# A decoder layer on one core: the norms' mean added with its sign turned, and a shorter run of filler products ahead of the first turn

## The chip, the cores and the metric

The kernel runs on one core of a Trainium2 chip. A core has a matrix engine (TensorE; PE in the profile, its weight loads PEld), VectorE (DVE), ScalarE (ACT), GpSimd (POOL) and a queue engine (SP) that here only issues transfers. The metric is the device time of one execution, in microseconds (us); lower is better. Several executions of a kernel are timed, and their median is given.

## The reference

One decoder layer on x of shape (4, 512, 128) in float32, 16 heads of 8 channels. Cut to what matters:

```python
def _layernorm(x, axis=-1, eps=1e-05):
    m = jnp.mean(x, axis=axis, keepdims=True)
    v = jnp.var(x, axis=axis, keepdims=True)
    return (x - m) / jnp.sqrt(v + eps)
...
x = x + attn(_layernorm(x))            # causal self-attention, Wq Wk Wv Wp with biases
x = x + xattn(_layernorm(x), ctx_1024) # attention to 77 context tokens, with a mask
x = x + ffn(_layernorm(x))             # 8 experts, the best 2 of each token weighted
```

The softmax subtracts each row's largest score. There are 3 norms for each of 4 batches, so 12 norms of 512 tokens each.

## The kernel before

Tokens lie on the 128 partitions, 4 tiles (T = 4) of 128 tokens for a batch; channels lie along the free dimension. One norm of one batch is this work:

- VectorE takes the statistics (BN_STATS and BN_AGGR into `moments`, which holds mean and variance, L740 and L743; L748 and L751 for the first norm).
- GpSimd adds the epsilon to the variance (`var`, L483), raises it to the power of minus one half (`rstd`, L484), and then writes `normed`, one instruction for each of the 4 tiles of tokens (L493). Each of these is `tensor_scalar` with two operations: subtract the mean, multiply by `rstd`. Both are one number per partition, read from memory.
- TensorE turns the 4 tiles (L884, `turn_x`), and ScalarE copies them out as `normed_t` (L613). Projections follow: q, k and v for the first norm of a batch, the query of the second attention, or the gate and the experts.

```python
last = gp.tensor_scalar(normed[:, i % 2, t], state[:, b, t], moments[:, n, t, 0:1],
                        rstd[:, n, t:t + 1], ALU.subtract, ALU.mult)
```

The very first norm (batch 0) is done in two halves of 2 tiles, `first_stats` to `first_split_k` for half 0 and half 1. The first half's `normed` is written by VectorE (L757), the second half's by GpSimd (L477). The turn of a half is L912, and its projections are L918.

Projected q and k are cut into three bfloat16 parts each (high, middle, low). The high part is ScalarE's; the rest after it is GpSimd's subtraction (L458); the middle is ScalarE's cast (L652); the low is GpSimd's subtraction again (L464). SP copies the parts into `q_stack` and `k_stack`, six transfers for each (L339), in the order high, middle, low. For batch 0 this is done by halves, on VectorE in GpSimd's place. A `peak` step multiplies the stacks on TensorE (L962 and L967), and VectorE finds each row's largest score (L781). A `scores` step multiplies again with that maximum inside (L1008). ScalarE takes the exponential (L672), GpSimd clears what lies above the diagonal (L569), and TensorE multiplies by the values (L1024). Before the first `scores`, SP has to put the maxima into `q_stack` (L415).

What sets the order: a string `ORDER` has one letter for each step. Every engine walks the whole string and does its own part of each step, in that order, with semaphores between engines. So each engine's program is in order, and an instruction that waits holds back all behind it. The letter `w` is a filler (`warm`): one product of ones with ones, 128x512 in bfloat16 (L893), into a bank that nobody reads. It does no work of the layer. There are 118 of them: 29 ahead of the first turn, 30 between the projection of the context keys and the first `peak`, the rest in small groups. GpSimd's early program is the clearing of buffers (`clear` steps, L500 to L523) between the norms.

Of the kernel before, what the change touches and what calls it, by code (L numbers as in the profile page):

```python
# [11 lines left out]
ALU = mybir.AluOpType  # L12
# [3 lines left out]
B, S, D, H, E = 4, 512, 128, 16, 8  # L16
DH = D // H
S2 = 77
T = S // 128
# [32 lines left out]
def chains():  # L52
# [34 lines left out]


ORDER = (
    "aqaqPVPPPwwwwwwwwwwwwwwwwwwwwwwwwwwwwwaLLLbwwaPLqaPwqwwaqbaVcqaqKwwwwwwwwwwwwwwwwwwwwwwwwwwwwwweeebe"  # L90
    "cebebebPebwweeewwbcKeewKKeKwwweeKiewwwwwKeeicecefwsLesiwwsfsfsafswfisfsfsfsvfsvfssvvfsjsvvmbsfsdvjsf"
    "svfscvvfsfvsfdsmvmcffscmdfsfmvfjsmsmLmvsggjvsgvsgmgsgmgsgvsmgvsgndggksdgvsgsvAkAsvAsnsAvgsAvAdsgvnAs"
    "AnAsggvdgnsgvsgAsvgsknshsnvcxhxvxkhxvhoynxhxyxhnEhshnhxhdsholsEnshsvlhsyshsvvBsBdyBPEsBvBPsEsBvBBBvs"
    "hoEhshoBEshsvEoEshxoxhsovxohxyxhxyFxvloElsoEsxFEvsvosssvpyyssvvFspsvCsFsCvCCCvvpCCFCEpFzCFzpCtpFptzx"
    "xtxpxzypFxxypFxFxGytGpyttGGFwwwwzwwwwDtDGDDtDDwDDDGzGtzDtztxGGxxGxGyxxyxxtHytyHtHGHwwzHztHtHztzHwwww"
    "wHwwwHHtttwwwwwwwwwwwwwwHwwwwzztttztztttt"
)


# [73 lines left out]
def decoder_layer(nc, x, ctx_t, mask, wq, bq, wk, bk, wv, bv, wp, bp, xwq, xwk, xwv, xwo,  # L173
                  gate_w, gate_b, expert_w, expert_b, out):
    with ExitStack() as stack:
        def sb(name, shape, dt=F32):
            return stack.enter_context(nc.sbuf_tensor(name, shape, dt))
# [26 lines left out]
        state = sb("state", [128, B, T, D])  # L204
        stats = sb("stats", [128, 3 * B, T, 6])
        moments = sb("moments", [128, 3 * B, T, 2])
        var = sb("var", [128, 3 * B, T])
        rstd = sb("rstd", [128, 3 * B, T])
        normed = sb("normed", [128, 2, T, D])
# [219 lines left out]
        def _(pool):  # L429
            gp = nc.gpsimd  # L430
            chain = [0]

            def link(ins):
                chain[0] += 1
                ins.then_inc(pool_chain, 1)
                pool.wait_ge(pool_chain, chain[0])
# [10 lines left out]
            for i in range(2):  # L447
# [3 lines left out]
                last = gp.affine_select(out=v, in_=v, compare_op=ALU.not_equal, fill=1.0, base=-64, pattern=[[-1, 64]],  # L451
                                        channel_multiplier=1)
# [14 lines left out]
            for step in SCHEDULE:  # L467
                kind, b, k = step
                if kind == "first_stats":
                    t = slice(2 * k, 2 * k + 2)  # L470
                    pool.wait_ge(first_moments_ready, k + 1)
                    link(gp.tensor_scalar(var[:, 0, t], moments[:, 0, t, 1], LN_EPS, None, ALU.add))
                    gp.tensor_tensor(rstd[:, 0, t], var[:, 0, t], minus_half[:, t], ALU.pow).then_inc(first_rstd_ready, 1)
                elif kind == "first_norm" and k == 1:
                    pool.wait_ge(first_rstd_ready, 2)
                    for t in (2, 3):
                        last = gp.tensor_scalar(normed[:, 0, t], state[:, 0, t], moments[:, 0, t, 0:1],  # L477
                                                rstd[:, 0, t:t + 1], ALU.subtract, ALU.mult)
                    last.then_inc(first_norm_ready[k], 1)
                elif kind == "ln_stats":  # L480
                    n = 3 * b + k
                    pool.wait_ge(moments_ready, STATS[step])
                    link(gp.tensor_scalar(var[:, n], moments[:, n, :, 1], LN_EPS, None, ALU.add))  # L483
                    link(gp.tensor_tensor(rstd[:, n], var[:, n], minus_half[:], ALU.pow))  # L484
                elif kind == "ln_norm":
                    n = 3 * b + k
                    i = NORM[step]
# [2 lines left out]
                    elif i > 2:  # L490
                        wait_full(pool, ("turn_x", *NORMS[i - 3][1:]))
                    for t in range(T):
                        last = gp.tensor_scalar(normed[:, i % 2, t], state[:, b, t], moments[:, n, t, 0:1],  # L493
                                                rstd[:, n, t:t + 1], ALU.subtract, ALU.mult)
                    last.then_inc(norm_ready, 1)
                elif kind == "clear" and k == "causal":

                    for rows in (128, 64):
                        v = causal[0:rows]
                        link(gp.memset(v, 0.0))  # L500
                        last = gp.affine_select(out=v, in_=v, compare_op=ALU.is_ge, fill=FUTURE, base=64 - rows,
                                                pattern=[[0, 4], [-1, 128]], channel_multiplier=1)
# [11 lines left out]
                elif kind == "clear" and k == "rank":  # L514
                    for e in range(E):
                        last = gp.memset(rank[:, :, e:e + 1], float(E - e))
# [612 lines left out]
```

## Time and profile before

| | us |
|---|---|
| median of 3 executions | 279.18 |
| lowest and highest of them | 278.38 and 280.3 |
| the execution that was profiled | 278.69 |
| its span, first to last instruction | 277.0 |
| TensorE busy | 258.9 (93% of the span) |
| VectorE busy | 207.6 (75%) |
| ScalarE busy | 162.7 (59%) |
| GpSimd busy | 150.5 (54%) |

The times of rows below are from the start of the span. The profiled execution took 1.7 us more than its span. It lies 0.5 us below the median. A row's "idle before" is how long its engine had nothing to run before the first instruction of the row, and the name behind it is what ended that. Ends of TensorE's products are modelled, so that neighbouring rows overlap by a tenth or two of a microsecond.

### The profile page before, as it was taken

Reading aid. Unit: us, or ns where it says so; the run is one execution under the profiler, and the core shown is the slowest. Engines: PE = TensorE matmul, PEld = TensorE weight load, DVE = VectorE, ACT = ScalarE, POOL = GpSimd, SP = SyncE. Lnnn points to the kernel's source line nnn. Section 1 sums busy time; section 2 is a strip of 40 time slices with the busy share of each in tenths; the row PEclk is TensorE's granted clock in tenths of the full one; section 3 lists DMA queues with packets and bytes.
Section 4 is the critical chain, followed back from the end, with each engine's and each line's share of the span. In section 5 each row is a group of like instructions: output and inputs, shape, how many; then the busy total and the mean of one; then the engine's idle time right before and its main releaser. Section 6 shows DMA issues by size and latency. Waiting matters only on the chain.

```text
span 277.0 us, 6747 instructions
## 1 busy us (share of the span) xinstructions
PE 258.9 (93%) x2642; PEld 140.3 (51%) x2642; DVE 207.6 (75%) x406; ACT 162.7 (59%) x223; POOL 150.5 (54%) x266
## 2 busy tenths in 40 slices
PE   8999896899988999999999969999799999998993
PEld 2554442434544444453545525367455684586583
DVE  6489997867887989987979945899338973864651
ACT  4232624989866988799977979961592009501100
POOL 7999833758869665675667694625811070032000
PEclk9999999799999999999999999999999999999999
DMA  3453364000452313400310001300004100100101
GB/s 106 110 143 94 86 165 110 2 6 4 117 152 71 82 37 105 135 9 5 100 31 2 7 2 29 98 2 8 0 11 116 38 7 2 38 2 0 38 2 39
DMA packets 21635, 14.62 MB, mean 53 GB/s; under 512 B 2788, under 2 KB 21604, under 8 KB 21604
## 3 DMA queue, kind: packets, MB, share of 16 engines
q1 hardware_dynamic: 20324, 13.61, 18.1%
q10 hardware_dynamic: 1280, 0.59, 0.8%
q8 instruction: 21, 0.34, 0.5%
q14 instruction: 10, 0.08, 0.1%
HBM read 2.39 MB, written 1.05 MB: 12 GB/s over the span
## 4 chain that ended last, share of the span: by engine, by line
PE 64%; DVE 17%; POOL 11%; ACT 3%; issue 2%; DMA 1%; POOLq 0%; SPq 0%; ACTq 0%
PE banks L1024 12%; POOL normed L493 8%; PE banks L1087 7%; PE banks L893 7%; PE banks L1008 7%; DVE peaks L781 6%; PE banks L884 5%; PE banks L967 4%; PE banks L1046 4%; PE banks L877 4%; PE banks L962 3%; DVE xpeaks L788 3%; POOL rstd L484 2%; PE banks L1073 2%; PE banks L1035 2%
## 5 line engine op out<-in xcount | busy, mean ns | idle before, releaser
L781 DVE TENSOR_REDUCE peaks<-banks 128x2 f32<-128x1024 f32 (+3 forms) x88 | 95.2, 1122 | 16.4 <-PE banks L967 15.8
L672 ACT ACTIVATE probs<-banks 128x1024 f32<-128x1024 f32 x80 | 79.4, 1031 | 14.3 <-PE banks L1008 13.7
L569 POOL TENSOR_SCALAR_AFFINE_SELECT probs<-probs 128x512 f32<-128x512 f32 (+1 forms) x80 | 43.2, 545 | 35.2 <-ACT probs L672 35.1
L1024 PE MATMUL banks<-probs,v_s 128*32 128x256 f32 (+3 forms) x512 | 43.2, 440 | 0.0
L677 ACT ACTIVATE xprobs<-banks 77x1024 f32<-77x1024 f32 x32 | 31.0, 1017 | 9.7 <-PE banks L1035 9.6
L493 POOL TENSOR_SCALAR normed<-state,moments,rstd 128x128 f32<-128x128 f32 x44 | 35.0, 809 | 0.7
L893 PE MATMUL banks<-ones_b 128*128 128x512 bf16 x118 | 32.1, 411 | 2.4 <-POOL minus_half L439 1.4
L1008 PE MATMUL banks<-q_stack,k_stack 64*128 64x512 bf16 (+3 forms) x256 | 30.8, 306 | 3.0 <-DMA q_stack<-peaks_t 2.4
L1087 PEld LDWEIGHTS banks<-expert_w_s,scaled 128*128 128x128 f32 x256 | 29.6, 192 | 4.9 <-issue 4.6
L1087 PE MATMUL banks<-expert_w_s,scaled 128*128 128x128 f32 x256 | 32.1, 280 | 0.0
L967 PE MATMUL banks<-k_stack,q_stack 64*128 64x512 bf16 (+3 forms) x256 | 31.9, 301 | 0.0
L851 DVE TENSOR_TENSOR scaled<-banks,normed_t 128x1024 f32<-128x1024 f32 x16 | 19.4, 1218 | 10.5 <-PE banks L1073 10.4
L962 PE MATMUL banks<-causal,halves 64*128 64x128 bf16 (+3 forms) x352 | 26.0, 227 | 1.0 <-DVE peaks L781 0.8
L788 DVE TENSOR_REDUCE xpeaks<-banks 128x8 f32<-128x616 f32 x32 | 23.9, 792 | 1.9 <-PE banks L983 1.6
L962 PEld LDWEIGHTS banks<-causal,halves 64*128 64x128 bf16 x352 | 13.3, 96 | 23.2 <-DVE peaks L781 10.4
L893 PEld LDWEIGHTS banks<-ones_b 128*128 128x128 bf16 x118 | 11.7, 104 | 17.4 <-issue 5.5
L1024 PEld LDWEIGHTS banks<-probs,v_s 128*32 128x32 f32 x512 | 12.3, 108 | 15.5 <-issue 11.4
L1008 PEld LDWEIGHTS banks<-q_stack,k_stack 64*128 64x128 bf16 x256 | 9.9, 96 | 16.3 <-DVE peaks L781 4.8
L1046 PE MATMUL banks<-xprobs,xv_s 77*32 77x512 f32 x128 | 16.6, 602 | 0.0
L613 ACT COPY normed_t<-banks 128x512 f32<-128x512 f32 x11 | 6.2, 586 | 16.3 <-PE banks L884 16.3
L807 DVE TENSOR_TENSOR g_scores<-banks,gate_b_s 128x32 f32<-128x32 f32 x4 | 0.8, 192 | 19.1 <-PE banks L877 19.1
L483 POOL TENSOR_SCALAR var<-moments 128x4 f32<-128x4 f32 x11 | 2.7, 246 | 22.4 <-DVE moments L743 22.3
(172 smaller groups left out, 370.8 us busy)
## 6 DMA issues: line engine op xcount, KB each, us to landing
xq_stack<-parts_x SPq DMA_DIRECT2D x24, 128.0 KB, 2.4
q_stack<-parts_q SPq DMA_DIRECT2D x18, 128.0 KB, 2.5
k_stack<-parts_k SPq DMA_DIRECT2D x18, 128.0 KB, 2.5
out<-state SPq DMA_DIRECT2D x4, 256.0 KB, 2.2
state<-in_x SPq DMA_DIRECT2D x3, 256.0 KB, 2.9
q_stack<-parts_q SPq DMA_DIRECT2D x12, 64.0 KB, 2.0
expert_w_s<-in_expert_w SPq DMA_DIRECT2D x1, 512.0 KB, 4.4
xk_stack<-parts_x SPq DMA_DIRECT2D x6, 77.0 KB
```

Source lines behind the costliest of these rows:

```text
L493: last = gp.tensor_scalar(normed[:, i % 2, t], state[:, b, t], moments[:, n, t, 0:1], rstd[:, n, t:t + 1], ALU.subtract, ALU.mult)
L569: gp.affine_select(out=v, in_=v, compare_op=ALU.is_ge, fill=0.0, base=0, pattern=pattern, channel_multiplier=-1).then_inc(causal_done, 1)
L672: ac.activation(probs[:, grp % 2, u], two_banks(step), ACT.Exp, scale=SCALE).then_inc(taken_by_act, 1)
L677: ac.activation(xprobs[0:S2, n % XPROBS], two_banks(step)[0:S2], ACT.Exp, scale=SCALE).then_inc(taken_by_act, 1)
L781: ve.tensor_reduce(peaks[:, f, t, :, a:a + n], two_banks(step)[:, :, 0:n * width].rearrange("p s (h k) -> p s h k", h=n), X_AXIS, ALU.max, ...
L788: ve.tensor_reduce(xpeaks[:, t, :, a:a + n], two_banks(step)[:, :, 0:n * S2].rearrange("p s (h k) -> p s h k", h=n), X_AXIS, ALU.max, nega ...
L893: te.matmul(bank(step), ones_b[:, 0:128], ones_b[:], start=True, stop=True)
L962: te.matmul(diagonal[:, s, :, 64 * i:128], halves[r, i], causal[r, 0:n, 0:128 - 64 * i], start=(i == 0), stop=False, skip_group_check=True)
L967: last = te.matmul(two[:, s, width * h:width * h + width], q_stack[r, b % 2, 4 * f + a + h, 128 * t:128 * t + 128], k_stack[r, b % 2, 4 * ...
L1008: last = te.matmul(two[:, s, col:col + n], k_stack[r, b % 2, p, 128 * kt:128 * kt + 128], q_stack[r, b % 2, p, 128 * kt:S], start=True, st ...
L1024: last = te.matmul(home[32 * c:32 * c + 32, 128 * kt:S], weight.rearrange("p a b -> p (a b)"), probs[:, half, unit, c % 2, col:col + S - 1 ...
L1087: last = te.matmul(home[:, D * t:D * t + D], scaled[:, (4 * b + k) % SCALED, i, 128 * t:128 * t + 128], expert_w_s[:, 2 * k + i], start=Fa ...
```

## The change

First, the norms. A new buffer `shift` holds the mean times minus one. GpSimd makes it with one more `tensor_scalar` for each norm, ahead of `var`, and for the second half of the first norm. `normed` on GpSimd is then `state` plus `shift`, times `rstd`: ALU.add stands where ALU.subtract stood, and `shift` where `moments` stood. 44 instructions in `ln_norm` and 2 in the second half of the first norm change so; 12 small ones are new. The first half's norm, on VectorE, stays.

Second, the fillers. `ORDER` without its `w` letters is the same string. Of the `w`, 15 of the 29 ahead of the first turn are gone, and so are 2 ahead of the last of the four first projections. New ones are 4 ahead of the turn of batch 1's first norm, 2 ahead of a pair of turns (the last norm of batch 1 and the second norm of batch 2), 1 ahead of the turn of batch 3's second norm, and 2 more (7 for 5) ahead of the turn of the last norm. 2 more have moved past a neighbouring step without a TensorE part. 118 become 110. No bank of a real step changes.

```diff
 ORDER = (
-    "aqaqPVPPPwwwwwwwwwwwwwwwwwwwwwwwwwwwwwaLLLbwwaPLqaPwqwwaqbaVcqaqKwwwwwwwwwwwwwwwwwwwwwwwwwwwwwweeebe"
...
+    "aqaqPVPPPwwwwwwwwwwwwwwaLLLbwwaPLqaPwqaqbaVcqaqKwwwwwwwwwwwwwwwwwwwwwwwwwwwwwweeewwwwbecebebebPebwwe"
...
+        shift = sb("shift", [128, 3 * B, T])
...
                     pool.wait_ge(first_moments_ready, k + 1)
+                    if k == 1:
+                        gp.tensor_scalar(shift[:, 0, t], moments[:, 0, t, 0], -1.0, None, ALU.mult)
...
                     for t in (2, 3):
-                        last = gp.tensor_scalar(normed[:, 0, t], state[:, 0, t], moments[:, 0, t, 0:1],
-                                                rstd[:, 0, t:t + 1], ALU.subtract, ALU.mult)
+                        last = gp.tensor_scalar(normed[:, 0, t], state[:, 0, t], shift[:, 0, t:t + 1],
+                                                rstd[:, 0, t:t + 1], ALU.add, ALU.mult)
...
                     pool.wait_ge(moments_ready, STATS[step])
+                    gp.tensor_scalar(shift[:, n], moments[:, n, :, 0], -1.0, None, ALU.mult)
...
                     for t in range(T):
-                        last = gp.tensor_scalar(normed[:, i % 2, t], state[:, b, t], moments[:, n, t, 0:1],
-                                                rstd[:, n, t:t + 1], ALU.subtract, ALU.mult)
+                        last = gp.tensor_scalar(normed[:, i % 2, t], state[:, b, t], shift[:, n, t:t + 1],
+                                                rstd[:, n, t:t + 1], ALU.add, ALU.mult)
```

Lines behind the edits lie 1 to 4 lower in the changed kernel: L893 becomes L897, L884 becomes L888, L493 becomes L497. TensorE's program at its start, in the kernel before:

```order
L893 MATMUL banks<-ones_b 128x512 x29
L912 MATMUL banks<-ident,normed 128x128 x2
L893 MATMUL banks<-ones_b 128x512 x2
L918 MATMUL banks<-normed_t,wq_s 128x256
L912 MATMUL banks<-ident,normed 128x128 x2
L918 MATMUL banks<-normed_t,wk_s 128x256
L893 MATMUL banks<-ones_b 128x512
L918 MATMUL banks<-normed_t,wq_s 128x256
L893 MATMUL banks<-ones_b 128x512 x2
L918 MATMUL banks<-normed_t,wk_s 128x256
```

The same place in the changed kernel:

```order
L897 MATMUL banks<-ones_b 128x512 x14
L916 MATMUL banks<-ident,normed 128x128 x2
L897 MATMUL banks<-ones_b 128x512 x2
L922 MATMUL banks<-normed_t,wq_s 128x256
L916 MATMUL banks<-ident,normed 128x128 x2
L922 MATMUL banks<-normed_t,wk_s 128x256
L897 MATMUL banks<-ones_b 128x512
L922 MATMUL banks<-normed_t,wq_s 128x256
L922 MATMUL banks<-normed_t,wk_s 128x256
```

29 products of ones have become 14, and the pair ahead of the last projection is gone; the 30 products a little later (not shown) stay. GpSimd's program from the first statistics on, in the kernel before:

```order
L472 TENSOR_SCALAR var<-moments 128x2
L473 TENSOR_TENSOR rstd<-var,minus_half 128x2
L477 TENSOR_SCALAR normed<-state,moments,rstd 128x128 x2
...
L483 TENSOR_SCALAR var<-moments 128x4
L484 TENSOR_TENSOR rstd<-var,minus_half 128x4
L513 MEMSET zeros_b 24x512
L513 MEMSET expert_b_s 32x512
L493 TENSOR_SCALAR normed<-state,moments,rstd 128x128 x4
```

And in the changed kernel:

```order
L474 TENSOR_SCALAR shift<-moments 128x2
L475 TENSOR_SCALAR var<-moments 128x2
L476 TENSOR_TENSOR rstd<-var,minus_half 128x2
L480 TENSOR_SCALAR normed<-state,shift,rstd 128x128 x2
...
L486 TENSOR_SCALAR shift<-moments 128x4
L487 TENSOR_SCALAR var<-moments 128x4
L488 TENSOR_TENSOR rstd<-var,minus_half 128x4
L517 MEMSET zeros_b 24x512
L517 MEMSET expert_b_s 32x512
L497 TENSOR_SCALAR normed<-state,shift,rstd 128x128 x4
```

One small instruction per norm is new, directly ahead of `var`, and nothing has changed places. The same holds for the other ten norms.

## Rows read from the trace of the kernel before

**Rows 1.** The page, part 1: busy us, share of the span, instructions.

```profile
PE 258.9 (93%) x2642; PEld 140.3 (51%) x2642; DVE 207.6 (75%) x406; ACT 162.7 (59%) x223; POOL 150.5 (54%) x266
```

**Rows 2.** Timeline, PE, first 24 us: start, us, what, idle before it.

```profile
1.37 9.33 PE L893 MATMUL banks<-ones_b 128*128 128x512 bf16 x29 [1.37 <-POOL minus_half L439]
10.54 0.38 PE L912 MATMUL banks<-ident,normed 128*128 128x128 f32 x2
...
15.72 6.64 PE L893 MATMUL banks<-ones_b 128*128 128x512 bf16 x30
22.29 0.50 PE L962 MATMUL banks<-causal,halves 64*128 64x512 bf16 x4
```

**Rows 3.** Timeline, PEld (weight loads of the same products), 5 to 13 us.

```profile
6.46 0.15 PEld L893 LDWEIGHTS banks<-ones_b 128*128 128x128 bf16 x1 [0.28 <-issue]
6.89 0.15 PEld L893 LDWEIGHTS banks<-ones_b 128*128 128x128 bf16 x1 [0.28 <-issue]
7.30 2.90 PEld L893 LDWEIGHTS banks<-ones_b 128*128 128x128 bf16 x14 [0.26 <-issue]
```

**Rows 4.** Timeline, all engines, 0 to 30 us: the early norms and the first peaks.

```profile
5.15 0.60 DVE L757 TENSOR_SCALAR normed<-state,moments,rstd 128x128 f32<-128x128 f32 x2 [0.53 <-POOL rstd L473]
...
6.25 1.59 POOL L477 TENSOR_SCALAR normed<-state,moments,rstd 128x128 f32<-128x128 f32 x2
...
18.57 3.75 POOL L493 TENSOR_SCALAR normed<-state,moments,rstd 128x128 f32<-128x128 f32 x4
...
23.05 17.45 DVE L781 TENSOR_REDUCE peaks<-banks 128x8 f32<-128x1024 f32 x17
...
23.71 0.66 PE L884 MATMUL banks<-ident,normed 128*128 128x128 f32 x4
...
24.64 3.13 POOL L493 TENSOR_SCALAR normed<-state,moments,rstd 128x128 f32<-128x128 f32 x4
...
28.46 1.16 POOL L458 TENSOR_TENSOR full_q<-full_q,parts_q 128x512 f32<-128x512 f32 x1 [0.69 <-ACT full_q L648]
```

**Rows 5.** Timeline, SP: transfers issued, 12 to 46 us.

```profile
12.66 3.83 SPq L339 DMA_DIRECT2D q_stack<-parts_q  x6
...
30.92 3.80 SPq L339 DMA_DIRECT2D q_stack<-parts_q  x6
...
40.23 4.00 SPq L339 DMA_DIRECT2D xk_stack<-parts_x  x6
44.27 1.54 SPq L415 DMA_DIRECT2D q_stack<-peaks_t  x2
```

**Rows 6.** Timeline, PE: the first scores.

```profile
47.12 0.39 PE L1008 MATMUL banks<-q_stack,k_stack 64*128 64x512 bf16 x2 [2.44 <-DMA q_stack<-peaks_t]
```

**Rows 7.** Groups of GpSimd's instructions by shape: busy us, mean ns | idle before.

```profile
L493 POOL TENSOR_SCALAR normed<-state,moments,rstd 128x128 f32<-128x128 f32 x44 | 35.0, 809 | 0.7
...
L555 POOL TENSOR_TENSOR xpeak_rest<-xpeaks,xpeak_parts 128x64 f32<-128x64 f32 x4 | 1.2, 306 | 0.3
...
L538 POOL TENSOR_TENSOR full_x<-full_x,parts_x 128x308 f32<-128x308 f32 x1 | 0.8, 768 | 0.1
...
L527 POOL COPY xprobs<-bv_s 128x128 f32<-128x128 f32 x1 | 0.3, 289 | 0.0
```

**Rows 8.** One line each, L483 and L493: ns min/median/max, first and last start.

```profile
L483 POOL TENSOR_SCALAR var<-moments x11: 227/232/393, 16.2 to 246.7; 128x4 f32<-128x4 f32 x11
...
L493 POOL TENSOR_SCALAR normed<-state,moments,rstd x44: 792/793/1208, 18.6 to 250.5; 128x128 f32<-128x128 f32 x44
```

**Rows 9.** Timeline, PE: every turn for which it stood idle on a norm.

```profile
76.96 0.63 PE L884 MATMUL banks<-ident,normed 128*128 128x128 f32 x4 [0.73 <-POOL normed L493]
...
88.60 0.66 PE L884 MATMUL banks<-ident,normed 128*128 128x128 f32 x4 [1.15 <-POOL normed L493]
...
165.55 1.06 PE L884 MATMUL banks<-ident,normed 128*128 128x128 f32 x8 [2.00 <-POOL normed L493]
...
200.07 1.06 PE L884 MATMUL banks<-ident,normed 128*128 128x128 f32 x8 [1.49 <-POOL normed L493]
...
229.09 0.63 PE L884 MATMUL banks<-ident,normed 128*128 128x128 f32 x4 [0.18 <-POOL normed L493]
...
251.31 0.66 PE L884 MATMUL banks<-ident,normed 128*128 128x128 f32 x4 [0.76 <-POOL normed L493]
```

More of the change, by code:

```diff
@@ L89 @@
 ORDER = (
-    "aqaqPVPPPwwwwwwwwwwwwwwwwwwwwwwwwwwwwwaLLLbwwaPLqaPwqwwaqbaVcqaqKwwwwwwwwwwwwwwwwwwwwwwwwwwwwwweeebe"
[L91 to L96, printed above, removed]
+    "aqaqPVPPPwwwwwwwwwwwwwwaLLLbwwaPLqaPwqaqbaVcqaqKwwwwwwwwwwwwwwwwwwwwwwwwwwwwwweeewwwwbecebebebPebwwe"
+    "eewwbcKeewKKeKwwweeKiewwwwwKeeicecefwsLesiwwsfsfsafswfisfsfsfsvfsvfssvvfsjsvvmbsfsdvjsfsvfscvvfsfvsf"
+    "dsmvmcffscmdfsfmvfjsmsmLmvsggjvsgvsgmgsgmgsgvsmgvsgndggksdgvsgsvAkAsvAsnsAvgsAvAdsgvnAsAnAsggvdgnsgv"
+    "sgAsvgsknshsnvcxhxvxkhxvhoynxhxyxhnEhshnhxhdsholsEnshsvlhsyshsvvBsBdyBPEsBvBPsEsBvBBBvshoEhshoBEshsv"
+    "EoEshxoxhsovxohxyxhxyFxvloElsoEsxFEvsvosssvpyyssvvFspsvCsFsCvCCCvvpCCFCEpFzCFzpCtpFptzxxtxpxzywwpFxx"
+    "ypFxFxGytGpyttGGFwwwwzwwwwDtDGDDtDDwDDDGzGtzDtztxGwGxxGxGyxxyxxtHytyHtHGHwwzHztHtHztzHwwwwwwwHwwwHHt"
+    "ttwwwwwwwwwwwwwwHwwwwzztttztztttt"
 )
```

## The prediction, written before the changed kernel was timed

> **What bounds the kernel now.** I read the page's busy times first. TensorE is busy for 93% of the span, 18.1 us idle in all [rows 1]. So a gain is either TensorE work that goes, or one of its waits that shortens. I then looked for those waits in three places.
>
> The front. In TensorE's timeline the reader is to see a block of 29 products of ones from 1.37 us, and the first turn only at 10.54 [rows 2]. Both halves of the norm that this turn and the next need are done long before: VectorE's half at 5.75, GpSimd's at 7.84 [rows 4]. So nothing but the fillers holds the first turn.
>
> The way from there to the first scores. SP issues its first copy into the stack at 12.66 and has hardly a gap until 44.27, when it issues the maxima [rows 5]. TensorE, idle for 2.44 us, takes them up at 47.12 [rows 6]. So the first scores come when SP has worked off its list, and that list begins with the first projection. VectorE's peaks begin at 23.05 [rows 4], and they follow the same front.
>
> The norms. From 76 us on there are six places where TensorE stood idle until GpSimd had written a norm: 0.73, 1.15, 2.00, 1.49, 0.18 and 0.76 us, together 6.31 [rows 9]. A norm is four instructions of 793 ns [rows 8], 3.17 us.
>
> **The fillers in front.** The weight loads of these products stand 0.43 us apart until 6.89; from 7.30 on 14 of them take 2.90 us, 0.21 apart [rows 3]. So TensorE ran at its lower level (1.2 GHz) for the first 14 products, which took about 14 x 0.427 = 6.0 us, and at 2.4 GHz for the other 15, which took 3.2 us. These 15 go. If the clock rises at the same moment, 14 products end at 1.37 + 6.0 = 7.35, and the first turn starts 3.2 us earlier. The norm's second half would then be needed at about 8.7 (3.2 before the second turn), and it is ready at about 8.1. SP's own list of loads is done early enough, since its first copy waited for ScalarE's first part. So SP's list starts 3.2 us earlier. The two products ahead of the fourth projection (0.43 us) are worth nothing by themselves: ScalarE and SP set the pace there, and the 30 fillers that follow only end earlier.
>
> The 4 new fillers (0.86 us) ahead of batch 1's turn cost nothing for the end while VectorE has the three peaks before them to work through. In the kernel before it needs 17.45 / 17 = 1.03 us for each [rows 4]. Those cover them.
>
> **The small instruction.** `shift` has the shape and kind of `var`, 232 ns [rows 8]. I take 0.23 us for each of the twelve. It stands on the path only where TensorE waits for a norm that itself follows its statistics directly: one at 88.60, two at 165.55 and two at 200.07 (two norms in a row), one at 229.09, one at 251.31. That is 7 x 0.23 = 1.6 us. At 76.96 GpSimd had done its statistics long before, so `shift` is hidden.
>
> **The norm instruction.** No row shows GpSimd add one number per partition and multiply by another. Its price is bounded from both sides. Above, it stays 793 ns [rows 8]; I see no reason for an addition to cost more than a subtraction. Below, it is a plain pass over 128 numbers, the copy's 289 ns [rows 7]. Which is it nearest to? Subtractions of two tensors took 306 ns for 64 numbers and 768 for 308 [rows 7], so 1.89 ns for a number, and 306 + 64 x 1.89 = 427 ns for 128, although they read twice as much. The norm goes through one tensor and takes 793. Set beside the 232 ns of a nearly empty one it spends (793 - 232) / 128 = 4.4 ns on a number, against 1.9 for two streams. So this pair of operations runs far off the pace of the other rows, and that is what speaks for a pair-dependent, slow form that the new pair may leave. What speaks against it is that the operand layout (one tensor, two numbers per partition) stays, and that may be the slow part as well. I give the first a little more than even odds and take 0.43 us, the row of the subtraction, as its size.
>
> The Trainium skill (GPSIMD Engine Reference, section on engine selection) says that elementwise work with one input runs "roughly line-rate" on GpSimd. By that rule a norm instruction would be near the copy's 289 ns already. The trace disagrees for the subtracting form, with 793 ns. If the rule holds for the adding form, each would be 0.14 us shorter than I take; the sum below would not change by it, since the idle times already limit the gain.
>
> **The sum for a faster norm.** Four instructions save 4 x (0.79 - 0.43) = 1.46 us, less 0.23 for `shift`: 1.2 us for each norm in a chain. No place gives back more than its idle time, and new fillers eat into it (0.21 us each):
>
> - 76.96: 0.73 of 0.73
> - 88.60: 1.15 of 1.15
> - 165.55, two norms, 2.4 saved: 2.00 of 2.00
> - 200.07, two norms, 2.4 saved: 1.49, less 0.43 for two fillers, 1.06
> - 229.09: 0.18, less 0.21 for one filler, nothing
> - 251.31: 0.76, less 0.43, 0.33
>
> That makes 5.3 us. TensorE's other idle time, 18.1 - 6.3 = 11.8 us, shows that it often meets another wait, so I let three quarters of it reach the end: 3.9. That share is a choice. With the front: 278.7 - 3.2 - 3.9 = 271.6 for an execution like the profiled one, and 272.0 for the median, which stood 0.5 above it. GpSimd's work ahead of SP's list gets shorter in this case, so nothing there takes the front's gain back.
>
> **Rivals.** (1) The norm is no faster. Then the change does half of what it could, and the front loses too. GpSimd is busy without a gap there. Batch 1's norm ended at 22.32 [rows 4]; two `shift` put it to 22.8. TensorE comes to that turn at 23.71 - 3.6 + 0.9 = 21.0 and waits 1.8 us. Batch 2's norm ended at 27.77 and now ends at 28.5, just when GpSimd took up `full_q` before (28.46) [rows 4]. Its low part of q comes about 3 x 1.16 later, at 31.9. SP issued the transfer that needs it as the last of the six from 30.92 on, at about 34.1 [rows 5]; 3.2 earlier would be 30.9. So SP gains 2.2, not 3.2. All together 278.7 - 2.2 + 1.6 = 278.1, and 278.6 for the median. The new fillers are hidden here in idle time. (2) A norm at some 600 ns: 4 x 0.19 - 0.23 = 0.5 saved on each, about 2.6 at the six places, and 2.8 in front: 273.8. I count it to the faster case. (3) Slower: the clock does not rise at 7.35. In the trace it rose after 6.0 us of unbroken products [rows 3], and now the products end at that very moment; behind them come turns and projections with waits between. If it rises only within the block of 30, the 3.4 us of front work take some 3 us more, and 14 of the 30 take 0.21 more each, 3.0. Against the gain of 3.6 TensorE is then 2.4 late, and with the `shift` 278.7 + 2.4 + 1.6 = 282.7, or 283.2 for the median. It decides as soon as the loads behind the first turn still stand 0.43 apart. For it speaks that the margin is nothing; against it, that only short waits lie behind (half a microsecond), and the clock stayed up over the same ones before.
>
> **How the numbers follow.** A measurement here tells about 1% (2.8 us) from no change. Chances: faster norm 0.50, norm no faster 0.37, slow clock 0.08, and 0.05 for a mixture, such as a dearer norm with a good front. The faster case alone spans 269 (all idle time gives back, and a copy-like norm) to 275 (600 ns and half of it lost). The second case stands at 277 to 280. The range of 80% is 269 to 279.5: it holds the first case and most of the second. Faster by over 1% (under 276.4): 0.51. Within 1%: 0.38, the second case. Slower (over 282.0): 0.11, the clock and a few tenths of the rest.
>
> **What would show it.** The first turn at 7.3 to 7.5 and SP's first copy near 9.5 show the front. The duration of `normed` settles the cases: 793 says rival 1, 290 to 450 says the forecast. In the forecast TensorE no longer stands idle before the turn near 158 (165.55 less 7), and the first scores start near 43.9; in rival 1 near 44.9, with 2.5 us of idle time at the pair of turns near 165. If the norm is fast and the time is still above 275, the idle time went to other waits, and my three quarters is the wrong step.

## The result, and the profile after

The changed kernel takes 271.94 us in the median of four executions (270.48 to 272.25), the kernel before 279.74 beside it (278.38 to 282.4). The ratio is 0.970, with a 95% interval of 0.962 to 0.978: faster by 3%. A later comparison on another occasion gave 0.971 (0.966 to 0.975). Medians here are over all executions; ratios leave out those that took over 1.5% more than the fastest of their kernel.

The page of the changed kernel, parts 1 and 4 (busy us, share, instructions; the chain that ended last):

```profile
span 268.5 us, 6731 instructions
...
PE 253.7 (94%) x2622; PEld 139.0 (52%) x2634; DVE 207.9 (77%) x406; ACT 162.8 (61%) x223; POOL 137.4 (51%) x278
...
PE 71%; SPq 13%; DVE 7%; issue 2%; POOL 2%; ACT 1%; DMA 1%; POOLq 0%; ACTq 0%
```

The chain of the kernel before, for comparison:

```profile
PE 64%; DVE 17%; POOL 11%; ACT 3%; issue 2%; DMA 1%; POOLq 0%; SPq 0%; ACTq 0%
```

By the page TensorE has 268.5 - 253.7 = 14.8 us of idle time left where it had 18.1 [rows 1]. That is too much: there are 2634 weight loads and only 2622 products, and the 12 products without a record are all fillers. At 0.21 us each they are 2.6 us, so about 12.2 us are left (an estimate). GpSimd had 11% of the chain before and has 2% now. SP's issuing of transfers, which had almost none, has 13%.

The norm's line in the changed kernel (ns min/median/max, first and last start), which answers to [rows 8], and the new small instruction:

```profile
L497 POOL TENSOR_SCALAR normed<-state,shift,rstd x44: 437/447/454, 19.8 to 242.3; 128x128 f32<-128x128 f32 x44
...
L486 POOL TENSOR_SCALAR shift<-moments x11: 243/250/392, 16.5 to 239.2; 128x4 f32<-128x4 f32 x11
```

A norm instruction takes 447 ns where it took 793. The small one takes 250. The four of a norm in a row take 1.74 us (from 24.07), where they took 3.13 (from 24.64) [rows 4], so the gain is not only in the recorded length of one.

TensorE's timeline at its start, and the turns that answer to [rows 2, 9] (start, us, idle before):

```profile
1.37 4.69 PE L897 MATMUL banks<-ones_b 128*128 128x512 bf16 x14 [1.37 <-POOL minus_half L440]
6.29 0.41 PE L916 MATMUL banks<-ident,normed 128*128 128x128 f32 x2 [0.24 <-DVE normed L761]
...
11.42 6.64 PE L897 MATMUL banks<-ones_b 128*128 128x512 bf16 x29
17.99 0.50 PE L966 MATMUL banks<-causal,halves 64*128 64x512 bf16 x4
...
21.55 0.66 PE L888 MATMUL banks<-ident,normed 128*128 128x128 f32 x4 [1.10 <-POOL normed L497]
...
44.61 0.39 PE L1012 MATMUL banks<-q_stack,k_stack 64*128 64x512 bf16 x2 [3.71 <-DMA q_stack<-peaks_t]
...
73.79 0.60 PE L888 MATMUL banks<-ident,normed 128*128 128x128 f32 x4
...
84.32 0.66 PE L888 MATMUL banks<-ident,normed 128*128 128x128 f32 x4
...
159.27 1.06 PE L888 MATMUL banks<-ident,normed 128*128 128x128 f32 x8
...
192.67 1.04 PE L888 MATMUL banks<-ident,normed 128*128 128x128 f32 x8
...
221.64 0.60 PE L888 MATMUL banks<-ident,normed 128*128 128x128 f32 x4 [0.16 <-issue]
...
243.40 0.60 PE L888 MATMUL banks<-ident,normed 128*128 128x128 f32 x4
```

The block of 30 products shows as 29, as one of them has no record. The same holds for the one filler just before the first scores: its weight load is at 40.83, so about 0.3 us of the 3.71 us of idle time was a product.

None of the six turns waits for GpSimd any more. The start of each, taken from the start of the same instruction in the kernel before, gives the lead that the changed kernel has at that point. Beside each turn stands the lead at the last row of mix or mixed turned before it:

| place (start before) | lead ahead of it | lead at it | gained | idle before it was |
|---|---|---|---|---|
| first scores (47.12) | | 2.51 | 2.51 | 2.44, now 3.71 (about 3.4 less the product) |
| turn at 76.96 | 2.28 | 3.17 | 0.89 | 0.73 |
| turn at 88.60 | 3.20 | 4.28 | 1.08 | 1.15 |
| two turns at 165.55 | 4.28 | 6.28 | 2.00 | 2.00 |
| two turns at 200.07 | 6.29 | 7.40 | 1.11 | 1.49 |
| turn at 229.09 | 7.43 | 7.45 | 0.02 | 0.18 |
| turn at 251.31 | 7.43 | 7.91 | 0.48 | 0.76 |

The last addition on VectorE comes 7.97 us earlier, and the span is 8.5 shorter; the half microsecond between is the last store, after which nothing else happens. So the norms gave 5.6 us, the front 2.3 (0.2 of its 2.5 was gone by 53 us, in a stretch of low clock). VectorE's starts have the same leads, 2.28, 3.20, 4.28, 6.29, 7.42 and 7.97 us, and step at the same places.

The kernel before had such a stretch too, with a granted clock of 0.57 from 48 to 52 us, after its own 2.44 us of idle time; the change did not bring it.

SP's timeline in the changed kernel, which answers to [rows 5]:

```profile
8.86 0.43 SPq L365 DMA_DIRECT2D state<-in_x  x1
9.40 4.07 SPq L340 DMA_DIRECT2D q_stack<-parts_q  x6
...
19.39 2.64 SPq L340 DMA_DIRECT2D k_stack<-parts_k  x3
...
28.55 3.82 SPq L340 DMA_DIRECT2D q_stack<-parts_q  x6
...
37.88 3.85 SPq L340 DMA_DIRECT2D xk_stack<-parts_x  x6
41.77 1.53 SPq L416 DMA_DIRECT2D q_stack<-peaks_t  x2
```

And one row of the kernel before:

```profile
22.35 1.88 SPq L339 DMA_DIRECT2D k_stack<-parts_k  x3
```

In the changed kernel SP's first copy comes 3.26 us earlier, right behind its own list of loads, which ends at 9.29. The first six copies took 4.07 us for 3.83. The three transfers from 19.39 on took 2.64 us to issue where they had taken 1.88: one took 1.36 us, the others 0.60. Behind them SP leads by 2.2 us, and by 2.4 to 2.5 from 23.64 on.

### The profile page after: what moved, and what is told of

Same layout as the page of the kernel before. It is cut to its first block, busy times and chain, and to the rows that moved or that the text cites. A ratio compares the mean times of both kernels' runs of the same rounds, so it can differ in the third digit from the quotient of the medians.

```text
span 268.5 us, 6731 instructions
## 1 busy us (share of the span) xinstructions
PE 253.7 (94%) x2622; PEld 139.0 (52%) x2634; DVE 207.9 (77%) x406; ACT 162.8 (61%) x223; POOL 137.4 (51%) x278
## 4 chain that ended last, share of the span: by engine, by line
PE 71%; SPq 13%; DVE 7%; issue 2%; POOL 2%; ACT 1%; DMA 1%; POOLq 0%; ACTq 0%
PE banks L1028 14%; PE banks L1091 10%; SPq L340 8%; PE banks L1012 7%; PE banks L888 6%; PE banks L881 5%; PE banks L1050 5%; PE banks L971 4%; PE banks L897 4%; PE banks L966 4%; PE banks L1077 3%; PE banks L1039 2%; PE banks L987 2%; DVE peaks L785 2%; PE banks L939 2%
## 5 line engine op out<-in xcount | busy, mean ns | idle before, releaser
L676 ACT ACTIVATE probs<-banks 128x1024 f32<-128x1024 f32 x80 | 79.5, 1031 | 15.2 <-PE banks L1012 14.8
L897 PE MATMUL banks<-ones_b 128*128 128x512 bf16 x98 | 26.7, 403 | 3.3 <-POOL minus_half L440 1.4
L497 POOL TENSOR_SCALAR normed<-state,shift,rstd 128x128 f32<-128x128 f32 x44 | 19.1, 447 | 0.8
L897 PEld LDWEIGHTS banks<-ones_b 128*128 128x128 bf16 x110 | 10.5, 102 | 16.2 <-issue 4.0
L486 POOL TENSOR_SCALAR shift<-moments 128x4 f32<-128x4 f32 x11 | 2.9, 262 | 23.9 <-DVE moments L747 23.3
```

The source lines that it names most:

```text
L676: ac.activation(probs[:, grp % 2, u], two_banks(step), ACT.Exp, scale=SCALE).then_inc(taken_by_act, 1)
L897: te.matmul(bank(step), ones_b[:, 0:128], ones_b[:], start=True, stop=True)
```

## The experiments

**One part alone.** `e1_norm_only` is the changed kernel with the old string of steps:

```diff
-    "aqaqPVPPPwwwwwwwwwwwwwwaLLLbwwaPLqaPwqaqbaVcqaqKwwwwww
+    "aqaqPVPPPwwwwwwwwwwwwwwwwwwwwwwwwwwwwwaLLLbwwaPLqaPwqwwaqbaVcqaqKwwwwww
...
```

> The changed kernel with the old ORDER: the norms add the negated mean, but 29 products of ones stand ahead of the first turn, and none of the new fillers is there. My account of the two traces says that the norms alone give back TensorE's six idle times (5.6 us of 6.3), so 279.5 - 5.6 = about 274, with the first turn at 10.5 and the first scores near 47. Rival: the norms were only worth it together with the earlier front (GpSimd's early work being what holds SP), then this stands above 276.

274.1 us, a ratio of 0.978 (0.973 to 0.982). That is the expected time, and 6.2 us less than the kernel before beside it. In its profile none of the six turns waits for a norm. But that execution is not the kernel before with faster norms alone. TensorE's clock rose earlier, so that the first turn came at 9.48 and not at 10.54, and the first scores at 45.96; 0.40 us of this lead was left at 53 us. At the places of [rows 9] it gained 0.89, 1.06, 1.99, 1.55, nothing that stayed, and 0.93 us, 6.4 in all. From 227 to 236 us it lost 3.2 us again, with TensorE busy throughout and a granted clock of 0.52 from 228 to 234. So the norms by themselves give back all of the idle time, 6.3 us.

`e2_order_only` is the kernel before with the new string:

```diff
-    "aqaqPVPPPwwwwwwwwwwwwwwwwwwwwwwwwwwwwwaLLLbwwaPLqaPwqwwaqbaVcqaqKwwwwww
+    "aqaqPVPPPwwwwwwwwwwwwwwaLLLbwwaPLqaPwqaqbaVcqaqKwwwwww
...
```

> The kernel before with the new ORDER: norms subtract the mean (793 ns), fillers as changed, no shift instruction. My account: the front is worth 2.3 us in the changed kernel, where SP's list starts 3.3 earlier and loses 0.8 on one slow transfer. Here GpSimd is late with batch 1's and batch 2's norms, so SP should be held to about 2.2 or less: 277 to 278 us. TensorE's idle times before the turns from 77 us on stay (6 us in all, less the new fillers). Rival: the front gives its full 3.3 us (below 276.5), or nothing (above 279), because what binds before the first scores is GpSimd and not SP's list.

The ratio is 0.994 (0.991 to 0.998), 1.6 us less than the kernel before beside it. The median of its ten executions, 279.06, is above the expected 277 to 278, but that was set against a kernel before at 279.2 and this one stood at 280.39. The gain expected was 1.2 to 2.2, and it was within that; in the profiled execution the lead stays at 1.9 to 2.0 us from 53 us to the end. The turns in its timeline:

```profile
22.50 0.66 PE L884 MATMUL banks<-ident,normed 128*128 128x128 f32 x4 [2.00 <-POOL normed L493]
44.95 0.39 PE L1008 MATMUL banks<-q_stack,k_stack 64*128 64x512 bf16 x2 [2.86 <-DMA q_stack<-peaks_t]
74.99 0.63 PE L884 MATMUL banks<-ident,normed 128*128 128x128 f32 x4 [0.74 <-POOL normed L493]
86.65 0.66 PE L884 MATMUL banks<-ident,normed 128*128 128x128 f32 x4 [1.16 <-POOL normed L493]
...
163.63 1.06 PE L884 MATMUL banks<-ident,normed 128*128 128x128 f32 x8 [2.04 <-POOL normed L493]
198.09 1.09 PE L884 MATMUL banks<-ident,normed 128*128 128x128 f32 x8 [0.89 <-POOL normed L493]
...
249.39 0.65 PE L884 MATMUL banks<-ident,normed 128*128 128x128 f32 x4 [0.35 <-POOL normed L493]
```

The idle times of [rows 9] are all there, less what new fillers now fill: 1.49 has become 0.89, and 0.76 has become 0.35. The first scores come at 44.95, 2.2 us earlier than before, where the prediction's rival 1 had put them (2.2), but not for its reason. It had SP wait for GpSimd's low part of q. SP's rows:

```profile
19.46 2.32 SPq L339 DMA_DIRECT2D k_stack<-parts_k  x3
...
28.27 3.80 SPq L339 DMA_DIRECT2D q_stack<-parts_q  x6
...
33.72 4.46 SPq L339 DMA_DIRECT2D k_stack<-parts_k  x6
```

The six copies of q took 3.80 us without a break, as before. What was lost of the first 3.28 us is in slow issues: 0.3 us in the first six, 0.44 at 20.11 and 0.65 at 36.93.

So the front and the norms add up within their intervals: 0.6% and 2.2% alone, 3.0% together.

**What makes a norm instruction slow.** `e3_add_mean` is the changed kernel without `shift`; the norms add the mean itself, so that its result is not a norm, and everything else is as it was:

```diff
-                    gp.tensor_scalar(shift[:, n], moments[:, n, :, 0], -1.0, None, ALU.mult)
...
-                        last = gp.tensor_scalar(normed[:, i % 2, t], state[:, b, t], shift[:, n, t:t + 1],
+                        last = gp.tensor_scalar(normed[:, i % 2, t], state[:, b, t], moments[:, n, t, 0:1],
                                                 rstd[:, n, t:t + 1], ALU.add, ALU.mult)
```

> The changed kernel without any shift instruction: GpSimd's norms add the mean itself (from the same two-number moments as before) and multiply; the sign of the mean in the output is therefore wrong. If the operation pair is what made the norm slow, L-normed stays at 447 ns although the operand is the old one; if the packed shift operand did it, it goes back to 793. The time, with twelve 0.25 us instructions fewer: no more than 0.3 us below the changed kernel, since TensorE no longer waits for the norms there except once, early; rival: 1.6 us below, as my sum of the seven small instructions on the path had it.

Its line of norms:

```profile
L493 POOL TENSOR_SCALAR normed<-state,moments,rstd x44: 441/452/493, 18.3 to 242.3; 128x128 f32<-128x128 f32 x44
```

The old operand, and still 452 ns: it is the operation, not where the number lies. The time, 272.29 us, ratio 0.970 (0.968 to 0.973), is that of the changed kernel. So the twelve small instructions cost nothing at the end. The wait for batch 1's turn was 0.25 us where the changed kernel has 1.10, but the first scores came at 44.39 against 44.61, since SP's list sets them.

`e5_forms` gives each of a norm's four instructions another pair of operations, so that its result is not a norm either (one execution, 275.43 us; its time is not used):

```diff
+                    gp.tensor_scalar(normed[:, i % 2, 0], state[:, b, 0], shift[:, n, 0:1],
+                                     rstd[:, n, 0:1], ALU.subtract, ALU.mult)
+                    gp.tensor_scalar(normed[:, i % 2, 1], state[:, b, 1], moments[:, n, 1, 0:1],
+                                     rstd[:, n, 1:2], ALU.add, ALU.mult)
+                    gp.tensor_scalar(normed[:, i % 2, 2], state[:, b, 2], rstd[:, n, 2:3],
+                                     shift[:, n, 2:3], ALU.mult, ALU.add)
+                    last = gp.tensor_scalar(normed[:, i % 2, 3], state[:, b, 3], rstd[:, n, 3:4],
+                                            shift[:, n, 3:4], ALU.mult, ALU.subtract)
```

> The changed kernel with four different operation pairs in the four tiles of each norm, so the output is not a norm: subtract then multiply (negated mean as operand), add then multiply (mean out of the packed moments), multiply then add, multiply then subtract. Each has its own line. If every pair with a subtraction is slow, lines one and four show 793 ns and lines two and three 447. If only a subtraction that comes first is slow, line four is at 447 too. If each pair has its own speed, all four differ.

The four lines, in the order of the code:

```profile
L496 POOL TENSOR_SCALAR normed<-state,shift,rstd x11: 800/806/808, 19.7 to 245.5; 128x128 f32<-128x128 f32 x11
...
L498 POOL TENSOR_SCALAR normed<-state,moments,rstd x11: 441/452/455, 20.5 to 246.3; 128x128 f32<-128x128 f32 x11
...
L500 POOL TENSOR_SCALAR normed<-state,rstd,shift x11: 441/454/457, 20.9 to 246.7; 128x128 f32<-128x128 f32 x11
...
L502 POOL TENSOR_SCALAR normed<-state,rstd,shift x11: 795/807/812, 21.3 to 247.1; 128x128 f32<-128x128 f32 x11
```

Both pairs with a subtraction take 806 ns, first or second; both with an addition take 453. The first of the expected outcomes.

**The new fillers.** `e4_no_new_fillers` leaves the nine out:

```diff
-    "...wwwwwweeewwwwbecebebebPebwwe...
+    "...wwwwwweeebecebebebPebwwe...
...
```

> The changed kernel without its 9 new fillers (4 before batch 1's turn, 2, 1 and 2 before three later turns). If they eat into the gain as my sum said, this is faster by about 0.2 us for each that stands on the path: 5 later ones, less those that lie in idle time, 0.6 to 1.1 us. If they lie in idle time, no difference (within 0.3 us). If they keep TensorE's clock up, slower than the changed kernel, with a lower granted clock.

270.24 us, ratio 0.965 (0.963 to 0.967), against 0.970 and 0.971 for the changed kernel: a difference of half a percent whose intervals touch. A second pair, `e6_sp_xk_late` and `e9_late_no_new` below, run beside each other, shows none (0.957 and 0.957). The traces of that pair say what medians cannot. From the two turns near 155 us to the end the kernel without the new fillers gains 0.8 us on the one with them: 0.4 at each of the two places where two are left out, and nothing where one is, since TensorE then waits 0.19 us right behind that turn. The traces of the changed kernel and of `e4_no_new_fillers` show the same 0.8 at the same places. So of the five later ones, 1.07 us in all, four cost their 0.8 us, now that nothing has to be waited for there. The four early ones cost nothing: without them TensorE waits longer for batch 1's norm, 1.59 us for 1.10.

Whether the fillers also keep the clock up stays open. In the first pair they do not: 0.985 to 0.992 of granted clock without them, 0.986 to 0.994 with them. In the second pair it is 0.987 to 0.998 without them and 0.992 to 1.000 with them, which would hide the 0.8 us in the medians.

**What binds the front.** `e7_front7` has 7 products of ones ahead of the first turn:

```diff
-    "aqaqPVPPPwwwwwwwwwwwwwwaLLLbwwaPLqaPwqaqbaVcqaqKwwwwww
+    "aqaqPVPPPwwwwwwwaLLLbwwaPLqaPwqaqbaVcqaqKwwwwww
...
```

> The changed kernel with 7 products of ones ahead of the first turn, not 14. In its trace the first turn already waited for VectorE's norm (at 6.29 us, idle 0.24), and SP's first copy at 9.40 comes right after its own load list, which ends at 9.29. So nothing is left to gain in front: the same time within 0.5 us, if the clock holds. If 7 products are too few to raise TensorE's clock, the first turns and projections run at half pace (their weight loads further apart) and SP's first copy comes after 10: slower by 1 to 3 us.

Its first rows on TensorE and its first copy on SP:

```profile
1.37 3.17 PE L897 MATMUL banks<-ones_b 128*128 128x512 bf16 x7 [1.37 <-POOL minus_half L440]
5.89 0.66 PE L916 MATMUL banks<-ident,normed 128*128 128x128 f32 x2 [1.36 <-DVE normed L761]
```

```profile
9.39 3.84 SPq L340 DMA_DIRECT2D q_stack<-parts_q  x6
```

The turn took 0.66 us where it had taken 0.38 to 0.41: TensorE was still at its lower level, as for all 7 products (3.17 us). SP's first copy came at 9.39 all the same. The ratio is 0.970 (0.964 to 0.976), the changed kernel's. So the first turn had time to spare, and a low clock there cost nothing in that execution: SP's list of loads, ending at 9.29, is what holds the front. `after_again` below says the same: there all 14 products ran at the lower level, the first turn came at 7.08, and SP's first copy at 9.40.

One of the four executions took 404.79 us, with a mean granted clock of 0.558, where every other execution of every kernel here has 0.966 or more. It is not in the ratio. Whether 7 products have a part in it was not tested, so "costs nothing" holds for the other three.

`e11_no_block` leaves the 30 products ahead of the first peaks out:

```diff
-    "...Kwwwwwwwwwwwwwwwwwwwwwwwwwwwwwweeewwwwbec...
+    "...Keeewwwwbec...
...
```

> The changed kernel without the 30 products of ones ahead of the first peaks; the 14 in front stay. TensorE then stands idle from about 11.5 to about 17.5 us. If these fillers only keep the clock, the granted clock falls in 12 to 24 us. VectorE needs 1.03 us for a peak, and three peaks took TensorE 1.4 us at full pace, so 0.95 each at half: VectorE stays the slower one and the end moves by less than 1 us. Rival: the low clock makes SP's side or the turn of batch 1 late, 1 to 4 us slower.

TensorE then stood idle for 5.44 us, until the transfers of the stack had landed, and went on at its lower level:

```profile
16.79 0.83 PE L966 MATMUL banks<-causal,halves 64*128 64x512 bf16 x4 [5.44 <-DMA k_stack<-parts_k]
```

```profile
12.00:18.00 6.00, 1.22 (x14) 0.94 (x16) 5.83 (x17) 1.29 (x3) 5.70 (x7) 0.81 0.73 175
18.00:24.00 6.00, 5.67 (x47) 3.07 (x42) 5.55 (x7) 1.03 (x2) 5.63 (x12) 0.62 0.31 78
```

(Windows of 6 us: length, busy time of PE, PEld, DVE, ACT and POOL, granted clock, share of the DMA engines, GB/s.) The granted clock is 0.81 and 0.62, and the time is 270.6 us, ratio 0.968 (0.961 to 0.974): no slower. Low clock in that stretch costs nothing measurable: SP's first copy is at 9.40 again, and the first scores come at 43.61, earlier than in the changed kernel. The rival, 1 to 4 us slower, falls.

**SP's list.** `e6_sp_xk_late` has SP issue the context keys after the first maxima:

```diff
-                elif kind == "split_context":
-
-                    copy_parts(sp, "x", 1, K_PARTS, xk_stack, slice(0, B * S2), xk_stacked)
...
                                      peaks_t[12 * s:12 * s + 12, k]).then_inc(max_stacked[k], 16)
+                    if (b, k) == (0, 0):
+                        copy_parts(sp, "x", 1, K_PARTS, xk_stack, slice(0, B * S2), xk_stacked)
```

> The changed kernel with one list moved: SP issues the six transfers of the context keys (3.85 us of its time) after the first maxima, not before them. In the changed kernel TensorE stood idle 3.71 us before the first scores, and ScalarE had the maxima ready at 38.0 while SP was busy until 41.7. If SP's list is what binds there, the first scores start near 41 and nothing else moves: 3.7 us less, and up to 1.7 more if the clock no longer falls after that idle time, so 266.5 to 268.5. Rival: something else is as late as SP (the stacks of batch 1, GpSimd), and the gain is under 1.5 us.

266.84 us, ratio 0.957 (0.952 to 0.961), 5.0 us below the changed kernel beside it (271.80). SP and TensorE in its timeline:

```profile
33.91 4.30 SPq L340 DMA_DIRECT2D k_stack<-parts_k  x6
38.25 1.54 SPq L413 DMA_DIRECT2D q_stack<-peaks_t  x2
39.83 3.79 SPq L340 DMA_DIRECT2D xk_stack<-parts_x  x6
```

```profile
41.24 0.39 PE L1011 MATMUL banks<-q_stack,k_stack 64*128 64x512 bf16 x2
```

The first scores start 3.4 us earlier and without idle time. Behind them the clock gives 0.5 us more. Windows of the changed kernel, and then of this one:

```profile
44.00:48.00 4.00, 3.39 (x30) 1.52 (x32) 1.41 (x2) 2.87 (x3) 1.24 (x4) 0.67 0.23 68
48.00:52.00 4.00, 3.37 (x41) 1.69 (x37) 4.00 (x5) 3.62 (x6) 3.40 (x6) 0.90 0.02 4
```

```profile
44.00:48.00 4.00, 3.26 (x43) 1.39 (x37) 4.00 (x4) 3.87 (x6) 3.60 (x9) 1.00 0.32 91
48.00:52.00 4.00, 3.41 (x46) 1.21 (x48) 3.24 (x5) 3.72 (x5) 2.65 (x6) 1.00 0.02 6
```

After the idle time the granted clock averaged 0.67 and 0.90; without it, it stays at 1.00. Between the two profiled executions (270.48 and 266.8) that is all. The medians differ by 5.0, since other executions of the changed kernel lose more to the clock: against `after_again` (272.16) the lead is 2.8 us at the first scores, 3.6 behind the low clock there, and 5.3 behind a second stretch of it at 184 to 188 us.

`e9_late_no_new` is the same without the nine new fillers.

> The same, and without the changed kernel's 9 new fillers. If these cost TensorE time on the path, 1 to 1.5 us below the kernel with them; if their cost was only seen between sessions, the same.

267.61 us, ratio 0.957 (0.953 to 0.962): the same as with them. The expected 1 to 1.5 us are missed; 0.8 us is seen in the trace only.

`e8_sp_all_late` moves the expert biases, the ones and the mask parts behind the first maxima too:

```diff
-                elif kind == "context_keys":
-                    wait_cleared(sp, "expert_b_s")
...
                     if (b, k) == (0, 0):
+                        wait_cleared(sp, "expert_b_s")
...
                         copy_parts(sp, "x", 1, K_PARTS, xk_stack, slice(0, B * S2), xk_stacked)
```

> The list moved further: SP issues also the expert biases, the rows of ones and the mask parts (11 transfers, 6.4 us of its time from 22.1 on) after the first maxima. With only the context keys moved, SP took up the maxima at 38.25, right after its last copy, and ScalarE had them ready at about 38.0. So SP's list was no longer what held them by more than 0.3 us, and this should be equal to that kernel, 266.8, within 0.7. Rival: batch 1's stacks come earlier and its peaks with them, 1 us or more faster.

A miss: 269.1 us, ratio 0.964 (0.958 to 0.969), about 2 us slower than with the context keys alone. The two ratios' intervals just overlap, but the traces show it: the second scores come 2.10 us later, and the lag stays to the end. Its timeline shows why:

```profile
45.78 4.37 SPq L340 DMA_DIRECT2D xk_stack<-parts_x  x6
```

```profile
53.70 0.39 PE L1010 MATMUL banks<-q_stack,k_stack 64*128 64x512 bf16 x2 [1.89 <-DMA q_stack<-peaks_t]
```

The list that was pushed back ends at 50.1, and the second pair of maxima waits behind it. The wait removed from one place came back at the next.

**The base, once more.**

> The changed kernel once more, beside the others on one chip: 271.9 within 0.5 us. It is the base for the two above, and its profile shows whether the granted clock after the idle time before the first scores varies from execution to execution (0.67 and 0.90 in 44 to 52 us before).

271.80 us. Its first turn, with all 14 products at the lower level:

```profile
7.08 0.38 PE L916 MATMUL banks<-ident,normed 128*128 128x128 f32 x2
```

It has the low clock at 44 us again (0.57), and one more:

```profile
44.00:48.00 4.00, 3.99 (x34) 1.67 (x36) 1.60 (x2) 2.97 (x3) 1.72 (x7) 0.57 0.20 60
...
184.00:188.00 4.00, 4.00 (x22) 4.00 (x22) 3.21 (x13) 0.00 (x0) 3.38 (x8) 0.57 0.04 12
```

## Why the prediction was right, and where it was not

**The norm instruction.** This was the doubtful price: 289 to 793 ns, with 427 taken. It is 447, and the reason given, a slow form that hangs on the pair of operations, is shown by `e3_add_mean` and `e5_forms`. The rate argument was the useful part: 4.4 ns for a number stood far off every other row. It could not tell which ingredient was slow, and the text said so with its even odds; that 0.43, a subtraction of two tensors, came within 0.02 of an addition and a multiplication of one is partly luck. On the rule that was weighed there (the Trainium skill, GPSIMD Engine Reference, engine selection, one input "roughly line-rate"): with 447 ns the adding form is still well above the copy's 289, so the trace does not agree with it for either form.

**What the norms give back.** The six places were taken as 0.73, 1.15, 2.00, 1.06, 0 and 0.33, 5.3 us. They gave 0.89, 1.08, 2.00, 1.11, 0.02 and 0.48, 5.6 (and 6.4 in `e1_norm_only`, without the new fillers). The step after that, "I let three quarters of it reach the end: 3.9", failed: all of it reached the end. The other waits took none of it back. The table of leads shows it: between the places the lead stays within 0.03 us, on TensorE and on VectorE. A likely reason, argued and not tested, is that the engines behind a turn had been pushed back by the same norm and moved with it.

**The front.** 3.2 us were predicted for SP's list, and 3.26 came. The text's margin, that SP's loads were "done early enough", was right by 0.1 us: in the profiled execution TensorE was ready a microsecond earlier still, and could not use it. Of the 3.2, 2.5 arrived at the first scores. One slow issue took 0.76; the first copies took 0.3 more, and the later rows gave 0.3 back. The step that failed is the word "nothing" in "nothing there takes the front's gain back": it was right of GpSimd and did not think of SP's own issues. All other kernels with the short front but one have such a slow issue too, in the copies to `k_stack` from 19 or from 33 us on. The one without, `e11_no_block`, has its first scores at 43.61, 3.5 us earlier than the kernel before. What makes an issue slow was not found.

These two misses, 1.7 us too little and 0.9 too much, cancelled in part. The prediction for an execution like the profiled one was 271.6, and it took 270.5. The median lies 1.5 above that, where 0.5 was allowed, so that 272.0 against 271.94 is luck: the sum was 1.1 us off.

**The small instruction.** 0.25 us for 0.23. The 1.6 us of the slow case was never tested, since the norms got faster; in this one it costs nothing that can be seen (`e3_add_mean`).

**An unforeseen wait.** The sum had no wait at the turn of batch 1. TensorE waited 1.10 us for it. GpSimd started that norm at 19.76, 1.2 us later than before (18.57). Of this 0.3 stood before that norm's own instructions, its `shift` is 0.46, and 0.4 came of `rstd` and a clear that took longer. It cost nothing, as `e3_add_mean` shows.

**The rivals.** Rival 1, a norm no faster, is close to what `e2_order_only` built: it predicted first scores at 44.9 (44.95 measured) and 0.6 us less than before; 1.6 less was measured, as no `shift` is in that kernel. Its 2.2 us for the front came out by luck: SP did not wait for GpSimd there, and slow issues took as much. Rival 2 has a slip in its sum: 278.7 - 2.6 - 2.8 is 273.3, not 273.8. Rival 3, the slow clock, did not come: the clock rose after 7 products in the profiled execution (their weight loads stand 0.43 apart up to 3.91 and from 4.33 on six take 1.23 us), not after 14 as in [rows 3]. In `after_again` it was the forecast's own case: all 14 at the lower level, the first turn at 7.08, and the clock up behind them. And rival 3's price was wrong. It was put at 6 us, 3 in the front work and 3.0 in the block of 30, and the executions of `e7_front7` and `e11_no_block` that were profiled had a low clock in that stretch and lost nothing, since SP sets the pace there.

## What to carry to other kernels

Compare an instruction's time per element with the other rows of its engine before accepting it: one that stands off by a factor of two is worth a try in another form with the same result. Here an in-order engine's idle time came back in full at every place; take a discount only where a row shows another wait that ends within it. Compare the starts of the same instructions in both traces, place by place: it shows what an agreeing total hides. And when a shortened front stops gaining, look for the queue that only issues: here its order, not its length, was worth 5.0 us on top, twice what the front had given, until the list moved too far.

## What the runs showed of the hardware

- On GpSimd, `tensor_scalar` over 128x128 float32 takes 447 to 454 ns with an addition and a multiplication in either order, and 793 to 807 with a subtraction in place of the addition.
- The moment at which TensorE's clock rises is not fixed by the program: after 14 products in one execution of the kernel before [rows 3], after 7 in one of the changed kernel, after all 14 in another of the same kernel (`after_again`).
- After idle times of 1.9 to 3.7 us before the first scores TensorE often ran at its lower level for some microseconds (granted clock 0.50 to 0.67 over 44 to 48 us in three kernels, 0.57 over 48 to 52 in the kernel before). Not always: `e11_no_block` after 2.50 us and `e8_sp_all_late` after 1.89 kept 1.00.
- The same happened with TensorE busy throughout by its records and no such idle time: in `after_again` at 184 to 188 us (0.57, 1.4 us lost), in `e1_norm_only` at 228 to 234 (0.52, 3.2 us) and in `e11_no_block` at 212 to 216 (0.50, 3.1 us). The cause stays open. Of the 1.7 us between the two profiled executions of the changed kernel, 1.4 arise there. The mean granted clock does not tell such executions apart by itself: 0.991 at 270.48 us and 0.986 at 271.93 to 272.25, but also 0.994 at 272.03. The kernel without the idle time has 1.000 in its best executions.
- One issue of a transfer in a row of equal ones took 1.36 us for 0.60. Every profiled kernel has at least one such of 1.0 to 1.95 us; the kernel before has its first at 71.19.
